# When the SP queue issues the packing loads of an attention kernel, and which engines compute its last inverse deviation

## The chip, the cores and the metric

The kernel runs on one core of one Trainium2 chip. The time is device microseconds of one execution. Each core has five engines with instruction queues of their own: TensorE (PE), VectorE (DVE), ScalarE (ACT), GpSimd (POOL) and SyncE (SP), which here only issues DMAs. Every queue is executed in order; a wait for a semaphore stops all that is queued behind it on that engine.

## The reference

One block for 4 x 1024 tokens of width 256: cross attention (16 heads of 16) over 77 context rows, then a mixture of 8 experts, top one, with a capacity of 640 tokens each.

```python
def reference(x, ctx_1024, mask, Wq, bq, Wk, bk, Wv, bv, Wo, bo, Wr, W1, W2):
    # attention: y = a @ W.T + b, 16 heads, masked softmax, output projection
    x = x + xattn(layernorm(x), ctx_1024, ctx_1024, mask, Wq, bq, Wk, bk, Wv, bv, Wo, bo)
    # experts
    t = layernorm(x).reshape(-1, 256)
    probs = softmax(t @ Wr); idx = argmax(probs); pmax = max(probs)
    pos = position of the token among those of its expert, in order of tokens
    kept = pos < 640
    comb = where(kept, relu(t @ W1[idx]) @ W2[idx], t)
    x = x + comb * where(kept, pmax, 1)
    return x
```

## The kernel before, in words

The tokens are cut into 8 groups (NG) of 512; LAST is 7. The first half of the kernel is a software pipeline over the groups (function `pipeline`): a step has the group `c` whose scores are computed, `n` = c + 1 whose row maxima are taken, `r` = c - 1 whose attention is projected, `o` = c - 2 that is routed, and `a`, `l`, `m` further ahead. The second half goes through the experts; it is TensorE's own work almost without a gap.

The scores of a group are taken in four **rounds** (k or r = 0 to 3). In each, PE multiplies (`scores`, L1439 and L1442), ACT takes the exponentials (L709), PE weighs the values (`weigh_values`, L1475), and ACT copies the unnormalised result of four heads from PSUM to `attnU` (`copy_attn`, L717). Of that strip SP issues three DMAs:

- `gather_sums` (L418) brings the 16 rows of sums of the exponentials to the tile `sums`;
- `store_strips` (L422) writes the whole strip, 256 KB, to DRAM (`strips`);
- `pack_strips` (L429) reads the useful half of it back into `attnC` (`attn_mem` in the trace), with the heads side by side. It must wait for the strip to have landed (`strip_stored`).

When the four gathers of a group have landed, DVE inverts the sums (`invert_sums`, L964), and in the next step SP spreads the reciprocals over the partitions with 8 DMAs (`spread`, L438). DVE multiplies (`normalise_attn`, L970), and PE takes the router's share and projects (`router_of_attn`, L1552, and `project`, L1527). `copy_attn` of round 0 of the next group waits for `sums_loaded` of all four rounds of this one, since it writes over the strip that they are read from; `weigh_values` of round 1 waits for that copy.

The last group (7) does not take this way: PE transposes its strips (`transpose_strips`, L1489, `transpose_back`, L1495).

At the end of the first half, each group's rows are sent to their expert's slots in DRAM. POOL computes the inverse deviation (`second_rstd`, L505 to L550: eight small instructions, with a power of -0.5 and one Newton step), writes it and the mean beside the rows, and issues four indirect DMAs (`dispatch`, L578). For groups 6 and 7 it does rstd, dispatch, rstd, dispatch in a row. DVE computes the slots of a group (`place`, L1075 to L1085), and from the totals the number of tiles of each expert (L1237, L1240), for which PE waits. PE then runs 36 products that keep it busy (KEEP_WARM, L1757), before it transposes the first expert's rows (`transpose_first_pair`, L1687). These come by SP's `load_first_slots` once all rows are sent, and DVE normalises them (L1194). ACT copies the transposed pair (L812), takes the exponential of the first logits (`raise_logits`, L808) and then the first ReLU (L796).

## Time and profile before

| | |
|---|---|
| median of 3 runs | 507.38 us (505.53 to 508.52) |
| the profiled execution | 504.69 us |
| its span, first to last instruction | 503.0 us |
| around the span | 1.69 us |
| PE busy | 463.8 us, 92% |
| DVE, ACT, POOL busy | 41%, 28%, 38% |
| mean granted clock of TensorE | 0.980 |

Times in rows are microseconds from the first instruction, so they add up to the span; a change of the span is set against 504.69, the time of the same execution, and then carried over to the median.

### The profile page before, as it was taken

The page shows a single profiled execution, that of the slowest core. Times are in us where ns is not written, and L with a number is a line of the kernel's source. Part 1 is how long each engine was busy: PE and PEld are TensorE (multiplying, and loading weights), DVE is VectorE, ACT ScalarE, POOL GpSimd, SP SyncE. Part 2 cuts the span into 40 slices and gives each one's busy share as a digit, 9 for nine tenths or more (in the row PEclk, how much of TensorE's full clock was granted, in tenths as well). Part 3 has the DMA queues.
Part 4 walks back from the last instruction along what each step waited for, and adds up shares of the span by engine and source line. Part 5 has one row for each costly group of instructions (what it writes and reads, how often), then busy time and mean ns, then how long its engine had stood idle before and what let it go on. Part 6 is the DMA issues. An engine that isn't in the chain of part 4 may idle for free.

```text
span 503.0 us, 8150 instructions
## 1 busy us (share of the span) xinstructions
PE 463.8 (92%) x3009; PEld 312.4 (62%) x3010; DVE 208.6 (41%) x607; ACT 140.7 (28%) x203; POOL 191.2 (38%) x336
## 2 busy tenths in 40 slices
PE   7999879989999989797947999999999999999995
PEld 3443425334443525142714889989999999899894
DVE  5877436667665646373631331131131131313211
ACT  1135344454535454437201220010010110102000
POOL 5742824465866271827474231101111111131212
PEclk9999999999999999899969999999999999999998
DMA  6998624542434252424115160060240340634000
GB/s 191 308 241 187 220 84 150 149 142 74 155 103 160 88 158 68 156 93 153 53 41 169 55 226 33 18 238 22 66 179 22 115 149 15 236 98 155 19 21 12
DMA packets 49950, 60.66 MB, mean 121 GB/s; under 512 B 4802, under 2 KB 40617, under 8 KB 49904
## 3 DMA queue, kind: packets, MB, share of 16 engines
q1 hardware_dynamic: 42224, 47.49, 31.1%
q0 software_dynamic: 3456, 7.35, 4.3%
q10 hardware_dynamic: 4224, 5.21, 3.4%
q8 instruction: 28, 0.46, 0.4%
q14 instruction: 18, 0.15, 0.1%
HBM read 31.79 MB, written 26.62 MB: 116 GB/s over the span
## 4 chain that ended last, share of the span: by engine, by line
PE 55%; DMA 24%; SPq 12%; issue 3%; POOL 3%; DVE 2%; ACT 1%; POOLq 0%; DVEq 0%; ACTq 0%
DMA strips<-shared 21%; PE tps L1719 11%; PE wk L1729 11%; PE tps L1739 11%; PE wk L1747 10%; SPq L438 6%; SPq L418 3%; SPq L429 3%; PE nat L1296 2%; PE wk L1350 2%; PE nat L1707 1%; PE nat L1417 1%; PE wk L1527 1%; POOL slot_rows L578 1%; PE wk L1475 1%
## 5 line engine op out<-in xcount | busy, mean ns | idle before, releaser
L669 POOL DMA_INDIRECT out_x<-attn_mem,dest x40 | 39.0, 975 | 182.6 <-DVE attn_mem L1261 179.9
L709 ACT ACTIVATE shared<-tps,mask_key 77x1024 f32<-77x1024 f32 x64 | 67.6, 1106 | 27.8 <-PE tps L1442 27.7
L941 DVE TENSOR_REDUCE rowmax<-nat 128x8 f32<-128x616 f32 x58 | 45.9, 791 | 49.2 <-PE nat L1417 49.2
L1729 PE MATMUL wk<-w_sb,shared 128*128 128x256 f32 x256 | 57.7, 379 | 0.0
L1719 PE MATMUL tps<-shared,w_sb 128*128 128x256 f32 x256 | 56.6, 379 | 0.8 <-ACT shared L812 0.8
L1739 PEld LDWEIGHTS tps<-shared,w_sb 128*128 128x128 f32 x480 | 56.0, 192 | 0.8
L1739 PE MATMUL tps<-shared,w_sb 128*128 128x128 f32 x480 | 56.0, 275 | 0.0
L1747 PE MATMUL wk<-w_sb,shared 128*128 128x256 f32 x240 | 54.3, 379 | 0.0
L1719 PEld LDWEIGHTS tps<-shared,w_sb 128*128 128x128 f32 x256 | 48.6, 190 | 7.5 <-issue 1.0
L1729 PEld LDWEIGHTS wk<-w_sb,shared 128*128 128x128 f32 x256 | 48.0, 190 | 6.2
L1417 PE MATMUL nat<-kblk,qT 64*128 64x308 f32 x232 | 46.3, 473 | 4.1 <-DVE rowmax L941 3.8
L1747 PEld LDWEIGHTS wk<-w_sb,shared 128*128 128x128 f32 x240 | 44.5, 190 | 5.4
L1261 DVE SCALAR_TENSOR_TENSOR attn_mem<-wk,gate,x_sb 128x256 f32<-128x256 f32 x31 | 15.0, 484 | 79.1 <-PE wk L1747 41.7
L1475 PE MATMUL wk<-shared,v_ones 77*32 77x512 f32 x256 | 34.9, 618 | 8.9 <-ACT shared L709 8.9
L1417 PEld LDWEIGHTS nat<-kblk,qT 64*128 64x128 f32 x232 | 18.3, 187 | 34.6 <-issue 34.4
L578 POOL DMA_INDIRECT slot_rows<-rows,slot x32 | 32.8, 1025 | 10.9 <-issue 9.3
L505 POOL TENSOR_SCALAR ln<-mv 128x4 f32<-128x4 f32 x16 | 4.0, 251 | 83.2 <-DVE mv L1036 59.5
L1442 PE MATMUL tps<-qT,kblk 32*77 32x512 f32 x256 | 34.2, 610 | 0.0
L802 ACT ACTIVATE shared<-tps 128x512 f32<-128x512 f32 x15 | 9.0, 597 | 88.0 <-PE tps L1739 88.0
L1350 PE MATMUL wk<-xnT,wq_sb 128*128 128x512 f32 x64 | 31.4, 615 | 0.5 <-ACT xnT L689 0.3
L1250 DVE TENSOR_SCALAR shared<-tps 128x512 f32<-128x512 f32 x16 | 11.1, 692 | 46.0 <-PE tps L1719 46.0
L1255 DVE TENSOR_SCALAR shared<-tps 128x512 f32<-128x512 f32 x15 | 10.4, 692 | 46.3 <-PE tps L1739 46.3
(195 smaller groups left out, 556.8 us busy)
## 6 DMA issues: line engine op xcount, KB each, us to landing
w_sb<-in_w SPq DMA_DIRECT2D x12, 1024.0 KB, 8.8
strips<-shared SPq DMA_DIRECT2D x28, 256.0 KB, 3.8
slot_rows<-zeros SPq DMA_DIRECT2D x1, 5340.0 KB, 30.4
x_sb<-slot_rows SPq DMA_DIRECT2D x7, 667.5 KB, 4.4
x_sb<-in_x SPq DMA_DIRECT2D x8, 512.0 KB, 8.8
w_sb<-in_w ACTq DMA_DIRECT2D x4, 1024.0 KB, 7.5
out_x<-base SPq DMA_DIRECT2D x8, 512.0 KB, 3.8
attn_mem<-strips SPq DMA_DIRECT2D x28, 128.0 KB
```

The source lines that it names most:

```text
L578: pool.indirect_dma_start(slots_dram, bass.IndirectOffsetOnAxis(ap=slot[g % 2][:, j:j + 1], axis=0), rows[g % 2][:, j, :], None, bounds_ch ...
L669: pool.indirect_dma_start(out_rows, bass.IndirectOffsetOnAxis(ap=dest[n % 2][:, c:c + 1], axis=0), y_sb[n % 2][:, c, :], None, bounds_chec ...
L709: act.activation(probsT[0:SK, r % 2, 2 * i:2 * i + 2, :], tps[0:SK, 2 * i:2 * i + 2, :], ACT.Exp, bias=mask_key[:, g // GPB:g // GPB + 1]) ...
L941: dve.tensor_reduce(rowmax[:, j, :, m, :], nat_heads(g, k), AX.X, ALU.max).then_inc(rowmax_ready, 1)
L1350: last = pe.matmul(bank[:, :], wq_sb[:, k, m * P:(m + 1) * P], xnT[g % 2][:, k, :], start=(k == 0), stop=(k == KD - 1))
L1417: last = pe.matmul(dst, qT[g % 2][of, m, j * P:(j + 1) * P], kblk[of, b, m, :, :].rearrange("p (i r) k -> p i (r k)", i=2), start=True, st ...
L1442: last = pe.matmul(tps[0:SK, q, :], kblk[of, b, m, (q % 2) * 2 + par, :], qT[g % 2][of, m, :], start=False, stop=True)
L1475: last = pe.matmul(bank[q * QUARTER:(q + 1) * QUARTER, :], v_ones[:, g // GPB, h, :], probsT[0:SK, r % 2, q, :], start=True, stop=True)
L1719: last = pe.matmul(tps[:, quarter, f * two:(f + 1) * two], w1_sb[n % 2][:, k, at * P:(at + 1) * P], tT_slots[n % 2][:, k, 0:two], start=(k ...
L1729: last = pe.matmul(wk[(SC * n + c) % 2][:, 0:D], hidden[:, f, c * P:(c + 1) * P], w2_sb[n % 2][:, f, :], start=(f == 0), stop=(f == FC - 1))
L1739: last = pe.matmul(tps[:, half, f * P:(f + 1) * P], w1_sb[n % 2][:, k, at * P:(at + 1) * P], tT_slots[n % 2][:, k, c * P:(c + 1) * P], sta ...
L1747: last = pe.matmul(wk[(SC * n + c) % 2][:, 0:D], hidden[:, f, 0:P], w2_sb[n % 2][:, f, :], start=(f == 0), stop=(f == FC - 1))
```

## The change

SP's queue is reordered: the packing load of a round stands behind the gather and the store of the round after it, and that of round 3 at the head of the next step, ahead of `spread`. And for group 7 alone the inverse deviation no longer runs on POOL: DVE adds epsilon, ACT takes the square root and copies the mean into the rows, DVE takes a reciprocal and a Newton step, and POOL's `dispatch` waits for these two.

```diff
@@ sync
             def step(m, l, a, n, c, r, o):
                 if has(r):
+                    pack_strips(r, 3)
                     spread(r)
                 if has(o) and o > 0:
                     store_base(o - 1)
@@
                     for k in range(ROUNDS):
                         gather_sums(c, k)
                         store_strips(c, k)
-                        pack_strips(c, k)
+                        if k > 0:
+                            pack_strips(c, k - 1)
 
             pipeline(step)
+            pack_strips(LAST - 1, 3)
             spread(LAST - 1)
@@ gpsimd
             def dispatch(g):
 
-                wait(pool, rstd2_step, 8 * g + 8)
+                if g < LAST:
+                    wait(pool, rstd2_step, 8 * g + 8)
+                else:
+                    pool.wait_ge(last_rstd_ready, 1)
+                    pool.wait_ge(last_mean_ready, 1)
                 wait(pool, route_ready, g + 1)
@@
             second_rstd(LAST - 1)
             dispatch(LAST - 1)
-            second_rstd(LAST)
             dispatch(LAST)
@@ scalar
             copy_attn(LAST, 3)
             copy_back(1)
+            act.activation(std2[:, 0:1], averager[:, 0:1], ACT.Sqrt).then_inc(last_std_ready, 1)
             bias_logits(LAST)
+            act.wait_ge(last_var_ready, 1)
+            act.wait_ge(last_std_ready, 1)
+            act.activation(std2[:, :], var2[:, :], ACT.Sqrt).then_inc(last_std_ready, 1)
+            act.copy(rows[LAST % 2][:, :, MEAN], mv2[:, :, 0]).then_inc(last_mean_ready, 1)
@@ vector
             second_stats(LAST, 1)
             second_moments(LAST)
+            dve.wait_ge(moments2, NG)
+            dve.tensor_scalar(var2[:, :], mv2[:, :, 1], EPS, None, ALU.add).then_inc(last_var_ready, 1)
             masked_positions(LAST)
             place(LAST)
+            dve.wait_ge(last_std_ready, 2)
+            dve.reciprocal(y2[:, :], std2[:, :]).then_inc(last_rstd_step, 1)
+            dve.wait_ge(last_rstd_step, 1)
+            dve.tensor_tensor(yy2[:, :], var2[:, :], y2[:, :], ALU.mult).then_inc(last_rstd_step, 1)
+            dve.wait_ge(last_rstd_step, 2)
+            dve.scalar_tensor_tensor(rstd2[:, :], yy2[:, :], -0.5, y2[:, :], ALU.mult, ALU.mult).then_inc(last_rstd_step, 1)
+            dve.wait_ge(last_rstd_step, 3)
+            dve.scalar_tensor_tensor(rows[LAST % 2][:, :, RSTD], rstd2[:, :], 1.5, y2[:, :], ALU.add, ALU.mult
+                                     ).then_inc(last_rstd_ready, 1)
```

The queue of SP in one step, before: the four rounds of group 1 (L418 gather, L422 store, L429 packing load).

```order
L418 DMA sums<-shared 16x1x128 [waits rsum_ready,attnU_ready]
L422 DMA strips<-shared 128x512
L429 DMA attn_mem<-strips 64x1x512 [waits strip_stored0]
L418 DMA sums<-shared 16x1x128 [waits attnU_ready]
L422 DMA strips<-shared 128x512
L429 DMA attn_mem<-strips 64x1x512 [waits strip_stored1]
L418 DMA sums<-shared 16x1x128 [waits attnU_ready]
L422 DMA strips<-shared 128x512
L429 DMA attn_mem<-strips 64x1x512 [waits strip_stored2]
L418 DMA sums<-shared 16x1x128 [waits attnU_ready]
L422 DMA strips<-shared 128x512
L429 DMA attn_mem<-strips 64x1x512 [waits strip_stored3]
```

The same place of SP's queue now (lines are 5 further down: L423, L427, L434).

```order
L423 DMA sums<-shared 16x1x128 [waits rsum_ready,attnU_ready]
L427 DMA strips<-shared 128x512
L423 DMA sums<-shared 16x1x128 [waits attnU_ready]
L427 DMA strips<-shared 128x512
L434 DMA attn_mem<-strips 64x1x512 [waits strip_stored0]
L423 DMA sums<-shared 16x1x128 [waits attnU_ready]
L427 DMA strips<-shared 128x512
L434 DMA attn_mem<-strips 64x1x512 [waits strip_stored1]
L423 DMA sums<-shared 16x1x128 [waits attnU_ready]
L427 DMA strips<-shared 128x512
L434 DMA attn_mem<-strips 64x1x512 [waits strip_stored2]
L434 DMA attn_mem<-strips 64x1x512 [waits strip_stored3]
```

Each packing load went one gather and one store back; the last two stand together, right ahead of the 8 DMAs of `spread`.

DVE behind `place` of the last group, before: the last slots, then the number of tiles (`tiles_used`), then the first expert's rows.

```order
L1082 TENSOR_TENSOR slotf<-first,pos 128x4
L1084 COPY rows<-token_no 128x4 [waits place_step]
L1085 TENSOR_TENSOR slot<-slotf,past 128x4
L1237 TENSOR_SCALAR tiles_f<-wk 128x8 [waits totals_ps]
L1240 SCALAR_TENSOR_TENSOR tiles_f<-wk,tiles_f 128x8 [waits tiles_step]
L1240 SCALAR_TENSOR_TENSOR tiles_used<-wk,tiles_f 128x8 [waits tiles_step]
```

The same place of DVE now (`ln_0` to `ln_4` are var2, y2, yy2, rstd2, std2).

```order
L1098 TENSOR_TENSOR slotf<-first,pos 128x4
L1100 COPY rows<-token_no 128x4 [waits place_step]
L1101 TENSOR_TENSOR slot<-slotf,past 128x4
L1206 RECIPROCAL ln_1<-ln_4 128x4 [waits last_std_ready]
L1208 TENSOR_TENSOR ln_2<-ln_0,ln_1 128x4 [waits last_rstd_step]
L1210 SCALAR_TENSOR_TENSOR ln_3<-ln_2,ln_1 128x4 [waits last_rstd_step]
L1212 SCALAR_TENSOR_TENSOR rows<-ln_3,ln_1 128x4 [waits last_rstd_step]
L1264 TENSOR_SCALAR tiles_f<-wk 128x8 [waits totals_ps]
L1267 SCALAR_TENSOR_TENSOR tiles_f<-wk,tiles_f 128x8 [waits tiles_step]
L1267 SCALAR_TENSOR_TENSOR tiles_used<-wk,tiles_f 128x8 [waits tiles_step]
```

Four dependent instructions came in ahead of the number of tiles.

ACT at the end of the first half now (L728 is `copy_attn`, L732 `copy_back`, L743 `bias_logits`, L828 the first pair's copy). Before, the two table loads and the rows of L794, L798 and L799 are not there.

```order
L728 COPY shared<-wk 128x512 [waits sums_loaded,strip_stored3,attn_ps]
L732 COPY attn_mem<-nat 128x512 [waits attn_back_ps]
L794 ACT_TABLE_LOAD
L794 ACTIVATE ln_4<-averager 128x1
L743 ACTIVATE lgT<-tps,lg_bias 128x128 [waits lgT_ps]
L798 ACTIVATE ln_4<-ln_0 128x4 [waits last_std_ready,last_var_ready]
L799 COPY rows<-mv 128x4
L828 COPY shared<-nat 128x2x256 [waits tT_slots_ps]
L824 ACT_TABLE_LOAD
L824 ACTIVATE raised<-scaled 128x40 [waits scaled_ready]
L812 ACTIVATE shared<-tps 128x512 [waits hidden_ps0,tiles_ready]
```

A table for the square root is loaded ahead of the last `bias_logits`, and the exponential's again ahead of the first `raise_logits`.

## Rows read from the trace of the kernel before

**Rows 1.** The page's part 4: the chain that ended last, by line.

```profile
DMA strips<-shared 21%; PE tps L1719 11%; PE wk L1729 11%; PE tps L1739 11%; PE wk L1747 10%; SPq L438 6%; SPq L418 3%; SPq L429 3%; PE nat L1296 2%; PE wk L1350 2%; PE nat L1707 1%; PE nat L1417 1%; PE wk L1527 1%; POOL slot_rows L578 1%; PE wk L1475 1%
```

**Rows 2.** Timeline of SP, group 4 to 5: start, length, line, DMA.

```profile
146.34 0.54 SPq L429 DMA_DIRECT2D attn_mem<-strips  x1
146.93 0.56 SPq L418 DMA_DIRECT2D sums<-shared  x1
147.52 0.44 SPq L422 DMA_DIRECT2D strips<-shared  x1
...
152.08 5.19 SPq L438 DMA_DIRECT2D attn_mem<-rsum  x8
```

**Rows 3.** Timeline of ACT, same stretch; brackets: idle before, and what ended it.

```profile
144.21 0.59 ACT L717 COPY shared<-wk 128x512 f32<-128x512 f32 x1 [0.44 <-PE wk L1475]
...
151.09 0.59 ACT L717 COPY shared<-wk 128x512 f32<-128x512 f32 x1 [3.01 <-DMA sums<-shared]
```

**Rows 4.** Waits of PE over the whole span: total us, times, longest.

```profile
PE wk L1475 <- ACT shared L709: 8.9, 5, 2.7
```

**Rows 5.** Timeline of PE where the longest of these waits ends, group 6.

```profile
206.60 1.92 PE L1475 MATMUL wk<-shared,v_ones 77*32 77x512 f32 x8 [2.70 <-ACT shared L709]
```

**Rows 6.** Windows, one per group: length; PE, PEld, DVE, ACT, POOL busy; clock; DMA.

```profile
60.60:90.10 29.50, 26.84 (x186) 11.30 (x182) 13.66 (x33) 13.39 (x17) 11.06 (x16) 0.94 0.45 141
90.10:118.10 28.00, 25.27 (x197) 11.32 (x193) 16.98 (x52) 13.24 (x17) 16.37 (x27) 1.00 0.43 127
118.10:143.70 25.60, 25.40 (x197) 11.26 (x193) 17.39 (x52) 13.44 (x18) 19.64 (x35) 1.00 0.37 118
143.70:170.30 26.60, 25.64 (x200) 11.31 (x193) 15.52 (x46) 13.34 (x18) 12.13 (x24) 1.00 0.38 123
170.30:196.50 26.20, 23.88 (x173) 10.04 (x169) 14.53 (x42) 12.78 (x16) 12.13 (x24) 1.00 0.36 116
196.50:224.80 28.30, 23.60 (x169) 9.59 (x165) 14.91 (x42) 12.18 (x16) 15.83 (x28) 0.94 0.38 123
```

**Rows 7.** Timeline of DVE: the normalisation in two groups.

```profile
159.71 1.29 DVE L970 TENSOR_TENSOR attn_mem<-attn_mem 128x512 f32<-128x512 f32 x2 [0.28 <-DMA attn_mem<-rsum]
...
213.77 1.81 DVE L970 TENSOR_TENSOR attn_mem<-attn_mem 128x512 f32<-128x512 f32 x2
```

**Rows 8.** Timeline of SP in group 6: last store, then spread.

```profile
200.47 0.44 SPq L422 DMA_DIRECT2D strips<-shared  x1
...
204.90 5.19 SPq L438 DMA_DIRECT2D attn_mem<-rsum  x8
```

**Rows 9.** Timeline of POOL: last dispatch of group 6, first of group 7.

```profile
256.59 0.97 POOL L578 DMA_INDIRECT slot_rows<-rows,slot  x1 [0.30 <-issue]
...
261.28 1.12 POOL L578 DMA_INDIRECT slot_rows<-rows,slot  x1 [0.79 <-POOL rows L550]
```

**Rows 10.** Timeline of DVE: number of tiles, and the first expert's rows.

```profile
255.89 0.16 DVE L1237 TENSOR_SCALAR tiles_f<-wk 128x8 f32<-128x8 f32 x1
256.09 0.17 DVE L1240 SCALAR_TENSOR_TENSOR tiles_f<-wk,tiles_f 128x8 f32<-128x8 f32 x1
...
270.62 0.74 DVE L1194 TENSOR_SCALAR shared<-x_sb 128x256 f32<-128x256 f32 x2 [14.17 <-DMA x_sb<-slot_rows]
```

**Rows 11.** Timeline of PE: last logits, the warming products, the first transposes.

```profile
249.78 0.27 PE L1559 MATMUL tps<-ident,uT 128*128 128x128 f32 x1
...
259.20 10.44 PE L1757 MATMUL nat<-max_nat,ones 128*128 128x512 bf16 x35 [3.69 <-issue]
271.41 0.66 PE L1687 MATMUL nat<-ident,shared 128*128 128x128 f32 x4 [1.77 <-DVE shared L1194]
```

**Rows 12.** Timeline of ACT: the only table load, and the end of the first half.

```profile
7.09 1.28 ACT L694 ACT_TABLE_LOAD   x1 [7.09 <-issue]
...
246.73 0.59 ACT L721 COPY attn_mem<-nat 128x512 f32<-128x512 f32 x1 [2.97 <-PE nat L1495]
```

**Rows 13.** The chain in order of time: first products that need the first ReLUs.

```profile
280.63 3.46 PE wk L1729 x16
```

More of the change, by code:

```diff
@@ L167, in xattn_moe @@
         var1, y1, yy1, rstd1 = (sb(f"ln1_{i}", [P, TPG]) for i in range(4))
-        var2, y2, yy2, rstd2 = (sb(f"ln2_{i}", [P, TPG]) for i in range(4))
+        var2, y2, yy2, rstd2, std2 = (sb(f"ln2_{i}", [P, TPG]) for i in range(5))
         lgT = sb("lgT", [P, P])
@@ L304, in xattn_moe @@
         rstd2_step = sem("rstd2_step")
+        last_var_ready = sem("last_var_ready")
+        last_std_ready = sem("last_std_ready")
+        last_mean_ready = sem("last_mean_ready")
+        last_rstd_step = sem("last_rstd_step")
+        last_rstd_ready = sem("last_rstd_ready")
         averages_ps = sem("averages_ps")
```

## The prediction

> **What bounds the kernel now.** I read the chain that ended last first. Its largest single entry is no engine: 21% are stores of strips to DRAM, and with SP's own issue time (lines 438, 418, 429) it runs through SP's queue for most of the first half [rows 1]. So the next view is SP's timeline. There the queue never rests of its own accord: a packing load leaves, the next round's gather and store follow within 0.6 us each, and then SP stands still until that store has landed, since the packing load behind it needs it; after round 3 come 8 spreads, 5.19 us of issue [rows 2]. Who suffers? ACT copied round 3 of group 4 at 144.21 to 144.80, so the gather could have been issued at 144.85. It left at 146.93, behind the packing load of round 2. ACT's first copy of the next group waited for these sums until 151.09, 3.01 us [rows 3]. PE's waits show what reaches it: before `weigh_values` of round 1 it stood 8.9 us in 5 places, behind an exponential that was itself late behind that copy [rows 4], the longest time 2.70 us [rows 5]. The windows by group give the size: one group (the third) has no such wait and lasts 25.60 us with PE busy for 25.40, which is PE's floor; the others last 26.6 to 29.5, but for the fifth, which has less work [rows 6]. So PE and SP's loop are almost tied, and SP's loop is the one that is behind.
>
> **Part 1, the packing loads.** Nothing is removed: 28 gathers, 28 stores, 28 packing loads and 56 spreads are issued as before. What moves is the wait. SP now waits for the landing of strip k with the store of strip k + 1 already out, so two landings overlap, and the gather of round 3 finds the queue free. The packing of round 2, which now needs the issue of round 3, and that of round 3 come together ahead of the spreads.
>
> I place one group on this order, with group 4's times. Gather 144.85, store 145.4, packing of round 2 at 146.0 (its strip landed long ago); the strip of round 3 lands 3.9 us after its issue, which is what 147.52 and the spreads' start at 152.08, less one packing issue of 0.6, show [rows 2]: 149.3. Packing of round 3 until 149.9. The sums came 4.1 us after their gather, with a packing load in front of them [rows 2, 3]; so now by 149.0 at the latest, the reciprocal (0.9 us) by 150.5 once DVE has finished the maximum that it has in front. The spreads start at 150.5, not 152.08: 1.5 us earlier. They ended at 157.3 and DVE's normalisation, which waited 0.28 us for them, began at 159.71 [rows 7]. That chain has then 1.5 us to give, and PE asks for about 1.0. It is enough in groups 1 to 5.
>
> The gain by group, against the floor of 25.6 [rows 6]:
> - group 1: 29.5 - 25.6 = 3.9 us. PE was not busy for 29.50 - 26.84 = 2.7 us of it; the rest is clock: the window's clock is 0.94, so for a part of it PE ran at 1.2 GHz and not at 2.4. The stall gone, that goes too.
> - group 2: 28.0 - 25.6 = 2.4.
> - group 3: nothing.
> - group 4: 26.6 - 25.6 = 1.0.
> - group 5: it has no transposes of a further group, so the floor doesn't hold for it; I take its stall alone, which is what the other four leave of the 8.9 us [rows 4]: 8.9 - 2.7 (group 6) - about 2.5, 2.4 and 1.0 in groups 1, 2 and 4 = 0.3.
> - group 6: its stall is 2.70 [rows 5], and its clock 0.94 too: PE was busy for 23.60 us against 23.88 in group 5, though it has one `query` less (some 2.0 us), so 1.7 us of slow clock. 4.4 us in all. But here the chain of the spreads is the next to be late. The last store left at 200.47, the spreads at 204.90 [rows 8]; in the new order the copy of round 3 ended at 197.55, the sums are there by 201.7, DVE is free at 202.3 and has inverted them at 203.2. So the spreads gain 1.65 us. They landed some 2.3 us after their end (157.3 to 159.7, above), that is at 212.4, and the normalisation began at 213.77 [rows 7]: 1.35 of slack. So 3.0 us of the 4.4 can come.
>
> Sum: 3.9 + 2.4 + 1.0 + 0.3 + 3.0 = 10.6 us. Into group 7 nothing more is gained: its copy ends after SP has caught up, and the chain gather, sums, reciprocal, spreads is as long as before.
>
> What the overlap may cost: packing of round 2 now reads while strip 3 is written. The trace doesn't show this pair. Bounds: it costs nothing (the loads of one queue follow one another, and the 16 DMA engines were busy 36 to 45% of these windows [rows 6]), or as much as the part by which the packing load in front held the old gather, some 1 us per group (4.1 us for 8 KB). Half of it would fall into the slack of 0.5 us. I take 0; the upper end is 5 groups by 0.5, 2.5 us.
>
> **Part 2, the last inverse deviation.** On POOL the eight instructions and a semaphore gap lie between the last dispatch of group 6, which ends at 257.56, and the first of group 7 at 261.28. Now the next dispatch can follow as the others do, 0.30 us behind: 257.86, so 3.4 us earlier [rows 9]. DVE's chain is done by then: it begins where the tiles began, at 255.89, and takes a microsecond (below). Then DVE's first normalised rows start at 270.62 - 3.4 = 267.2 and the transposes could at 268.0.
>
> But PE isn't free then. It runs the warming products from 259.20 to 269.64, and the transposes came at 271.41 after 1.77 us of idle [rows 11]. And those products start when the number of tiles is known, for which DVE now has four dependent instructions and an addition in front. A dependent step of this size has a pitch of 0.20 us (255.89 to 256.09) [rows 10]: five of them, 1.0 us. The warming thus ends at 270.65, and the transposes gain 271.41 - 270.65 = 0.75 us, not 3.4. Bounds: -0.5 (steps of 0.3, each wait 0.1 more, and PE's slow clock longer after the longer rest) to 1.77 (the steps hidden). I take 0.7.
>
> ACT gets two table loads. The one row of such a load lasts 1.28 us [rows 12]. The first begins when `copy_back` ends at 247.32, so the table is there at 248.60, the dummy root at 248.8, and `bias_logits` ends by 249.2. PE takes its result at 249.78 [rows 11]: hidden, with 0.6 us to spare. The second stands behind the copy of the first pair (271.41 + 0.66 + 0.6 = 272.7) and ends at 274.0; the ReLUs behind it are needed at 280.63 [rows 13]: hidden by far.
>
> The trace's one load had nothing before it on ACT, so it doesn't show what a switch costs behind running work. The bounds are the one load, 1.28 us, and twice that, 2.56. I take the one load, as the row has it. The Trainium skill speaks against the change here: its page "ScalarE: Activation LUTs", section "What ACT_TABLE_LOAD costs", says that a switch to another set is the load and a drain of about 1.38 us, 2.66 in all. By that rule, as an estimate, the bias would end at 250.6, 0.8 us past the time at which PE takes it, and the part of the sum for the end of the first half would be 0.7 - 0.8 = -0.1; no row here has such a drain.
>
> **Sum.** 504.69 - 10.6 - 0.7 = 493.4 us for an execution like the profiled one. The median of the runs is 507.38, 0.53% above it; carried over, 496.0 us. That is 2.2% less.
>
> **Rivals.**
> - *A longer switch of tables.* At twice the row's load the table is there at 249.9, the dummy root at 250.1 and the bias at 250.5, 0.7 us after PE wants it; PE's two transposes and the projection behind them wait, and DVE's choice, the totals and the warming with them. For it: nothing in the trace excludes an ACT that stands between two tables. Against it: the one row has 1.28. 496.0 + 0.7 = 496.7 us. (The page's rule above is of this kind.)
> - *The packing chain takes over.* DVE and PE wait for the spreads in every group, because sums or strip 3 land later than I take; the spreads then start only some 0.5 us earlier. For it: the slack in group 4 was negative already, 0.28 us of wait [rows 7], and in group 6 I need this term myself. Against: strips landed in 3.9 us with a packing load ahead of them. Half of the gain goes: 501.0 us.
> - *The gather of round 3 is early, and nothing follows from it*, since PE is at its floor in any case and clock or a later wait eats what the stall gives. Then only a part of the two longest waits goes, 1 to 2 us: about 506, the middle of 504.5 to 508. Against it stand the windows: the group without a stall is the shortest of the full ones.
> - *Slower.* The pair of packing loads waits for a strip 3 that lands late because packing 2 reads beside it. It decides from a start of the spreads more than 7.9 us after the end of the copy (152.08 against 144.21 now). If the strip took 8 us, twice what it does, the spreads would start some 9.9 us after the copy, 2 us later than now, and PE would wait for it in six groups: 12 us more than now, less some 2 for the two longest of the old stalls: 507.4 + 10 = 517 us. Against it: in group 4 even a landing of 6 us would leave it level.
>
> **Chances.** My forecast 0.60, the longer table switch 0.14, the packing chain 0.13, nothing follows 0.07, slower 0.06. What a measurement of this kernel can tell from no change is about 0.5%, 2.5 us, so 504.8 to 509.9 is the same. The first three are faster: 0.87; of the fourth I count most as the same, and some of the slower case is small: faster 0.87, same 0.08, slower 0.05. The range: the sum's bounds are 2.5 us up for the overlap and 1.2 up, 1.0 down for the end; the full 1.4 us of group 6 may come after all, and the medians scatter by 1.5 us. That makes 491.5 to 500; to leave out no more than 2 in 10 it has to reach the packing chain's case: 491.5 to 502.
>
> **What would show it.** SP's timeline: the gather of round 3 within 0.1 us of the copy's end, and SP idle for some 8 us before it. PE's waits: the 8.9 us before `weigh_values` behind ACT gone or under 1. Windows of a group of 25.5 to 25.7 us, clock 1.00. In group 6 a wait of PE for the normalisation of about 1 us. At the end: warming products starting 4.4 us after DVE's last slots (3.4 now: 259.20 against 255.8) and the transposes right behind them with no idle, DVE's rows ready before. ACT's bias done before PE asks. It would be wrong if strip stores took over 5 us, if the groups stayed over 26 us without the ACT wait, or if the warming products ended later than 271.4 in the old frame.

## The result, and the profile after

| | before | after |
|---|---|---|
| median | 507.95 us (505.53 to 509.28, 4 runs) | 492.45 us (490.15 to 493.73, 4 runs) |
| the profiled execution | 504.69 us | 491.57 us |
| its span | 503.0 us | 489.8 us |
| mean granted clock | 0.980 | 0.987 |

Ratio 0.9695, 95% interval 0.964 to 0.975: 3% faster. The forecast was 496.0 us with a range of 491.5 to 502. The span is 13.2 us shorter; the sum had 11.3. The same two kernels, run again later with more executions, gave 0.9742 (below). An execution over 1.5% above the fastest of its kernel stands in the range but is left out of the ratio, which concerns one run of one experiment and three of the kernel before beside it.

Part 4 of the page after, the chain that ended last by engine and by line:

```profile
PE 83%; DVE 9%; issue 3%; DMA 2%; SPq 1%; POOL 1%; ACT 1%; ACTq 0%; DVEq 0%; POOLq 0%
PE tps L1746 11%; PE wk L1756 11%; PE tps L1766 11%; PE wk L1774 11%; PE nat L1444 8%; PE wk L1377 5%; PE wk L1502 5%; PE tps L1469 5%; PE wk L1554 5%; DVE rowmax L957 2%; PE nat L1784 2%; PE tps L1466 2%; PE wk L1361 1%; PE nat L1734 1%; DMA mask_u<-in_mask 1%
```

The strips, 21% of the chain before [rows 1], are no longer among its entries. PE stands in their place.

A word on names. "Group 4" in the rows and here is the window from one maximum cast to the next, in which rounds 0 to 2 of group 4 run. Counted off, the gather and the copy of round 3 and the spreads that fall into it are those of group 3 (the first 16 of 28 gathers), and the normalisation too. Where a group itself is meant below, the text says so.

The timeline of SP in the window of group 4, and under it ACT's copy of round 3 there (start, length, line, operation; brackets: idle before and what ended it):

```profile
128.47 0.56 SPq L434 DMA_DIRECT2D attn_mem<-strips  x1
137.62 0.54 SPq L423 DMA_DIRECT2D sums<-shared  x1
138.19 0.44 SPq L427 DMA_DIRECT2D strips<-shared  x1
138.73 2.23 SPq L434 DMA_DIRECT2D attn_mem<-strips  x2
143.26 5.21 SPq L443 DMA_DIRECT2D attn_mem<-rsum  x8
```

```profile
137.00 0.58 ACT L728 COPY shared<-wk 128x512 f32<-128x512 f32 x1 [0.44 <-PE wk L1502]
```

and DVE's inversion of the sums:

```profile
142.30 0.93 DVE L980 RECIPROCAL rsum<-sums 64x128 f32<-64x128 f32 x1
```

SP was free from 129.03 and issued the gather 0.04 us after the copy's end (2.1 us late before, [rows 2, 3]). The two packing loads are one row: the first left at 138.73, the second, a packing issue long (about 0.55), at about 140.4, as soon as strip 3 had landed, 2.2 us after its store. Packing was over at 140.96, but the spreads start at 143.26, with the end of the reciprocal: 6.26 us after the copy's start, 7.87 before (152.08 against 144.21; the forecast's "7.9 us after the end of the copy" is counted from its start too).

The windows of groups 1 to 6, from one maximum cast of ACT (L715) to the next; columns as in [rows 6], where the last two are the share of the DMA engines and their GB/s:

```profile
59.73:84.99 25.26, 25.13 (x186) 10.91 (x189) 13.16 (x30) 13.47 (x17) 11.65 (x17) 1.00 0.59 194
84.99:110.31 25.32, 25.28 (x197) 11.36 (x200) 16.98 (x53) 13.47 (x18) 16.64 (x27) 1.00 0.39 129
110.31:135.98 25.67, 25.45 (x197) 11.28 (x200) 17.38 (x52) 13.46 (x17) 19.58 (x35) 1.00 0.38 127
135.98:161.29 25.31, 25.27 (x197) 11.35 (x200) 15.41 (x46) 13.47 (x17) 12.35 (x25) 1.00 0.39 128
161.29:186.60 25.31, 23.84 (x173) 10.03 (x177) 14.47 (x43) 12.99 (x16) 12.40 (x24) 1.00 0.38 123
186.60:214.23 27.63, 23.54 (x169) 9.73 (x173) 15.57 (x43) 12.31 (x16) 15.80 (x28) 0.94 0.35 114
```

Cut at the same casts, the kernel before had 29.46, 28.07, 25.64, 26.52, 26.23 and 28.34 us. The gains are 4.20, 2.75, 0, 1.21, 0.92 and 0.71: 9.8 us. Group 6 still has a clock of 0.94. Its rows on PE, and under them DVE's normalisation and POOL's addition of an output bias:

```profile
196.16 1.07 PE L1502 MATMUL wk<-shared,v_ones 77*32 77x512 f32 x8 [1.58 <-ACT shared L720]
197.15 0.48 PE L1466 MATMUL tps<-maxT,minus_piece 32*77 32x512 bf16 x4
197.41 1.93 PE L1469 MATMUL tps<-qT,kblk 32*77 32x512 f32 x8
...
205.59 0.65 PE L1579 MATMUL wk<-attn_mem,wowr_sb 128*32 128x128 f32 x16 [1.36 <-DVE attn_mem L986]
```

```profile
203.21 2.33 DVE L986 TENSOR_TENSOR attn_mem<-attn_mem 128x512 f32<-128x512 f32 x2
...
203.76 3.72 POOL L549 TENSOR_TENSOR x_sb<-x_sb,bo_sb 128x256 f32<-128x256 f32 x4
```

Two things stand out. L1469 takes 1.93 us for eight products that take 1.03 elsewhere: TensorE at 1.2 GHz instead of 2.4. And the normalisation takes 2.33 us where it takes 1.28 in the windows before, while POOL's addition runs beside it; PE waits 1.36 us for it. The end of the first half, on PE:

```profile
242.69 0.19 PE L1597 MATMUL wk<-onehot,before 128*128 128x32 bf16 x1 [1.16 <-DVE onehot L1079]
...
249.21 9.30 PE L1784 MATMUL nat<-max_nat,ones 128*128 128x512 bf16 x36 [3.82 <-issue]
258.34 0.60 PE L1714 MATMUL nat<-ident,shared 128*128 128x128 f32 x4
```

the same stretch on DVE (last slots, first and last step of the new chain, number of tiles, first rows):

```profile
245.69 0.23 DVE L1101 TENSOR_TENSOR slot<-slotf,past 128x4 int32<-128x4 f32 x1
245.76 0.17 DVE L1206 RECIPROCAL ln<-ln 128x4 f32<-128x4 f32 x1
...
246.38 0.17 DVE L1212 SCALAR_TENSOR_TENSOR rows<-ln,ln 128x4 f32<-128x4 f32 x1
...
246.85 0.17 DVE L1267 SCALAR_TENSOR_TENSOR tiles_used<-wk,tiles_f 128x8 int32<-128x8 f32 x1
256.73 0.74 DVE L1221 TENSOR_SCALAR shared<-x_sb 128x256 f32<-128x256 f32 x2 [9.71 <-DMA x_sb<-slot_rows]
```

and on ACT:

```profile
236.38 0.58 ACT L732 COPY attn_mem<-nat 128x512 f32<-128x512 f32 x1 [2.98 <-PE nat L1522]
236.98 1.28 ACT L794 ACT_TABLE_LOAD   x1
238.28 0.20 ACT L794 ACTIVATE ln<-averager 128x1 f32<-128x1 f32 x1
238.38 0.35 ACT L743 ACTIVATE lgT<-tps,lg_bias 128x128 f32<-128x128 f32 x1
```

Against the kernel before, PE is 10.04 us earlier at the last cast, 10.35 at L1597, 9.99 at the first warming product and 13.07 at the transposes [rows 11]. The stretch from the first warming product to the transposes is 9.13 us instead of 12.21: the warming takes 9.30 instead of 10.44, and the 1.77 us of idle behind it are gone. So from L1597 on the end gives 2.7 us, and the rest of the program 0.1: 13.2 in all.

### The profile page after: what moved, and what is told of

The parts are those of the page before. It is cut to its first block, busy times and chain, and to the rows that moved or that the text cites. A ratio compares the mean times of both kernels' runs of the same rounds, so it can differ in the third digit from the quotient of the medians.

```text
span 489.8 us, 8154 instructions
## 1 busy us (share of the span) xinstructions
PE 459.0 (94%) x3010; PEld 311.9 (64%) x3010; DVE 209.7 (43%) x612; ACT 144.3 (29%) x208; POOL 189.5 (39%) x328
## 4 chain that ended last, share of the span: by engine, by line
PE 83%; DVE 9%; issue 3%; DMA 2%; SPq 1%; POOL 1%; ACT 1%; ACTq 0%; DVEq 0%; POOLq 0%
PE tps L1746 11%; PE wk L1756 11%; PE tps L1766 11%; PE wk L1774 11%; PE nat L1444 8%; PE wk L1377 5%; PE wk L1502 5%; PE tps L1469 5%; PE wk L1554 5%; DVE rowmax L957 2%; PE nat L1784 2%; PE tps L1466 2%; PE wk L1361 1%; PE nat L1734 1%; DMA mask_u<-in_mask 1%
## 5 line engine op out<-in xcount | busy, mean ns | idle before, releaser
L1444 PEld LDWEIGHTS nat<-kblk,qT 64*128 64x128 f32 x232 | 18.4, 187 | 34.3 <-issue 34.0
L1469 PE MATMUL tps<-qT,kblk 32*77 32x512 f32 x256 | 33.8, 602 | 0.0
```

Of the source, the lines that this page charges most:

```text
L1444: last = pe.matmul(dst, qT[g % 2][of, m, j * P:(j + 1) * P], kblk[of, b, m, :, :].rearrange("p (i r) k -> p i (r k)", i=2), start=True, st ...
L1469: last = pe.matmul(tps[0:SK, q, :], kblk[of, b, m, (q % 2) * 2 + par, :], qT[g % 2][of, m, :], start=False, stop=True)
```

## The experiments

The kernel before was run again beside each set; ratios are to those runs, with 95% intervals. Edits are shown against the kernel after, cut at `...`. Each experiment has one trace; what is read from it is one execution.

**The order alone** (part 1 without part 2; the last deviation on POOL as before):

```diff
             dispatch(LAST - 1)
+            second_rstd(LAST)
             dispatch(LAST)
...
-            act.activation(std2[:, 0:1], averager[:, 0:1], ACT.Sqrt).then_inc(last_std_ready, 1)
...
-            dve.reciprocal(y2[:, :], std2[:, :]).then_inc(last_rstd_step, 1)
...
```

> SP's queue in the new order, the last inverse deviation on POOL as before. Theory A (the groups' stalls behind SP are 9.8 us of the profiled difference, the end 2.7 us, of which 1.8 is PE's idle before the first transposes): this gives 9.8 to 10.5 us against before, PE idles again some 1.8 us ahead of the first transposes, and group 6 still stands 1.6 us before weigh_values of round 1 with a slow clock behind it. Rival B (the order alone gives all of 13 to 15 us, and the end follows from it): the ratio is that of the full change, 0.970. Rival C (the two parts help each other, the order alone gives half): under 7 us.

Measured: 495.83 us (491.71 to 497.9), ratio 0.9819 [0.9768, 0.9871]. PE's wait for ACT's exponential before `weigh_values`, 8.9 us in 5 places before, is down to 1.6 us in one (L1478 in this kernel). The transposes come 12.16 us after the first warming product, as before (12.21). PE waits for the first rows at the end:

```profile
PE nat L1690 <- DVE shared L1197: 2.5, 1, 2.5
```

The order gives most of the gain, some 9 us of the median, and it alone leaves the end as it was: its warming products are over in 9.67 us, and PE then stands idle 2.5 us instead of 1.8. Group 6 takes 25.05 us at full clock behind the wait of 1.6 us; the slow clock that was expected there came in group 1, which takes 27.86 us.

**The root alone** (part 2 without part 1):

```diff
-                        if k > 0:
-                            pack_strips(c, k - 1)
+                        pack_strips(c, k)
...
```

> The last inverse deviation on DVE and ACT, SP's queue as before. Theory A: 2 to 3 us faster than before: the transposes follow the warming products without idle (1.8 us), these start 0.4 to 0.9 us later, and run 0.5 to 1.3 us shorter if PE's clock goes back to 2.4 GHz sooner. Rival D (0.7 us, as predicted; the rest of 2.7 us in the first comparison was chance of the clock): 0.3 to 1.0 us. No table switch is seen to cost more than 1.28 us.

Measured: 502.24 us (499.13 to 504.11, 12 runs), ratio 0.9957 [0.9927, 0.9987]: 0.4%, some 2 us. The idle behind the warming is gone here too; warming to transposes is 10.41 us instead of 12.21, 1.8 less, since the warming itself took 10.57. That fits the first theory, but the interval, 0.7 to 3.7 us, reaches down to the second. The trace also shows how the old order spends what PE gains elsewhere. PE in group 7:

```profile
236.62 0.82 PE L1576 MATMUL nat<-attn_mem,wowr_sb 128*32 128x128 f32 x16 [3.24 <-DVE attn_mem L983]
```

In this execution the windows of groups 2 to 6 took 25.3 to 25.7 us each, after a first one of 32.13 us (a wait of 3.87 and slow clock), and then PE met the normalisation of the real group 6 3.24 us too early. PE and SP's queue are nearly tied in the old order: PE can run at its own pace for some windows, and pays elsewhere. From the first spreads to the last, six windows on, it is 155.6 us here and 159.7 and 157.5 in the two traces of the kernel before; in the two of the full change it is 152.1 and 150.4. The last spreads start at 227.43, 230.17 and 225.85 in the old order, at 219.21 and 220.40 after the change.

**Only round 2's packing load deferred** (those of rounds 0 and 1 stay where they were):

```diff
-                        if k > 0:
-                            pack_strips(c, k - 1)
+                        if k < 2:
+                            pack_strips(c, k)
+                        if k == 3:
+                            pack_strips(c, 2)
```

> As the full change, but the packing loads of rounds 0 and 1 stand in their old place; only that of round 2 goes behind the gather and store of round 3, and that of round 3 to the next step. Theory A (what pays is that the gather of round 3 finds the queue free): as the full change within 0.5%, if SP can catch up during the 9 us before round 3; SP then has the old two landings in rounds 0 and 1, 4 to 5 us each, and is behind by 1 to 3 us at round 3 in the worst group. Rival E (the overlap of the landings of all rounds pays): only half of the 10 us of the order comes, and PE's waits behind ACT stay at 3 us or more.

Measured: 492.08 us (489.87 to 494.55), ratio 0.976 [0.9714, 0.9807], level with the full change. So the part of the order that pays is the one ahead of round 3. This kernel has both kinds of store in one group; SP's timeline in rounds 1 to 3 of the real group 6:

```profile
208.46 0.56 SPq L423 DMA_DIRECT2D sums<-shared  x1
209.06 0.44 SPq L427 DMA_DIRECT2D strips<-shared  x1
213.27 0.54 SPq L434 DMA_DIRECT2D attn_mem<-strips  x1
213.85 0.56 SPq L423 DMA_DIRECT2D sums<-shared  x1
...
217.75 0.45 SPq L427 DMA_DIRECT2D strips<-shared  x1
218.30 2.15 SPq L434 DMA_DIRECT2D attn_mem<-strips  x2
220.54 5.21 SPq L443 DMA_DIRECT2D attn_mem<-rsum  x8
```

The store at 209.06 had a packing load right ahead of its gather (207.85) and its own packing load went 4.2 us later. The store at 217.75 had none ahead for 4 us: 2.15 us, counting the second of the merged pair as the last 0.55 us of its row. The trace of the kernel before had such a pair too, which the forecast did not use. There the stores of round 0 of groups 1 and 2 stand behind spreads and a gather:

```profile
76.42 0.44 SPq L422 DMA_DIRECT2D strips<-shared  x1
78.55 0.54 SPq L429 DMA_DIRECT2D attn_mem<-strips  x1
```

2.13 us, and 2.17 in group 2; its round 3 stores of groups 1 to 5, each behind a packing load, took 3.7 to 4.8.

**The full change again:** no edit.

> The full change once more, on the chip and in the call of the three below. All theories: 12.5 to 15.5 us under before (ratio 0.970 to 0.976). Theory G (its runs fall into those in which PE's clock drops in group 6 behind its 1.6 us wait and those in which it doesn't): the runs with a mean clock of 0.990 or more are 2 to 4 us shorter than those with 0.986 or less.

Measured: 490.27 us (489.86 to 494.61), ratio 0.9742 [0.9694, 0.9791]. Four runs of mean clock 0.991 lie at 489.9 to 490.3, two of 0.984 and 0.982 at 493.2 and 494.6. The profiled one is slow elsewhere than the first: group 6 took 25.05 us at full clock, though PE waited the same 1.58 us there, and group 1 took 27.84. Windows of this execution (cut at round times), and DVE and POOL in its group 6:

```profile
58.50:86.30 27.80, 27.67 (x198) 10.97 (x198) 12.59 (x28) 13.59 (x17) 13.88 (x18) 0.88 0.47 157
187.00:212.50 25.50, 22.45 (x168) 9.67 (x169) 14.62 (x43) 12.32 (x15) 14.92 (x28) 1.00 0.39 128
```

```profile
205.44 1.28 DVE L986 TENSOR_TENSOR attn_mem<-attn_mem 128x512 f32<-128x512 f32 x2
...
207.60 2.77 POOL L549 TENSOR_TENSOR x_sb<-x_sb,bo_sb 128x256 f32<-128x256 f32 x4
```

PE is busy for nearly all of group 1, so the 2.6 us over the 25.26 of the other execution is clock and no wait. In group 6 the drop of the first execution costs 2.6 us too (27.63 against 25.05), but only 1.5 of it is PE at the slow clock. The other 1.0 is a wait: with PE late, DVE's normalisation began 16.6 us after the cast instead of 15.1 and came to lie beside POOL's addition, which began at 17.2 in both; PE stood 1.36 us before L1579 instead of 0.32. Over the thirteen traces the normalisation of this window took 1.81 to 2.36 us in the four in which the two overlap (both of the kernel before, that of the late store, and the first of the full change) and 1.28 or 1.29 in the nine in which they don't.

Where the clock drops can be counted over the nine traces that have the order of this change (two of the full change, seven of the experiments): in group 6 once, in the execution shown first; in group 1 three times (27.84, 27.86 and 27.78 us against 25.3); in the other five in neither. The mean clock with a drop in group 1 is 0.984 in the two kernels that also have the root, with one in group 6 0.987.

**Filling PE's last wait.** In group 6 there is no `query` to run while ACT takes the exponentials; ten warming products stand in:

```diff
                     if has(a):
                         query(a, 0, c)
+                    else:
+                        keep_warm(10)
                     weigh_values(c, 1, l, n, r, o)
```

> The full change with 10 products that compute nothing, put where group 6 has no query for PE, ahead of weigh_values of round 1. Theory G: PE's wait of 1.6 us there becomes 0 to 0.3, the group lasts as long as before (25.0 us) or 0.2 more where the clock held, and the runs with the low clock become rarer: median 0.5 to 2 us under the full change, clock of the group 1.00. Rival H (group 6 is bound by the spreads, as the prediction had it): PE's wait moves to the normalisation, and the clock drops there.

Measured: 491.58 us (490.23 to 492.98), ratio 0.9757 [0.9713, 0.9802]; the 0.5 to 2 us under the full change did not come. The wait went from 1.58 to 0.17 us and the group still took 25.05 us: products that only fill a wait shorten nothing, since ACT's exponential ends when it did. Three of six runs have a mean clock of 0.984 and no trace. That is the value of the traces with a drop in group 1, where this kernel changes nothing, so these runs do not say what the fill does to the clock of group 6. The three traces with the fill keep it there, but so do five of the six with the order and without the fill.

**Number of tiles ahead of the deviation** (DVE's four new steps moved behind L1267):

```diff
             place(LAST)
-            dve.wait_ge(last_std_ready, 2)
-            dve.reciprocal(y2[:, :], std2[:, :]).then_inc(last_rstd_step, 1)
...
+            dve.wait_ge(last_std_ready, 2)
+            dve.reciprocal(y2[:, :], std2[:, :]).then_inc(last_rstd_step, 1)
...
```

> The full change with DVE's three instructions for the number of tiles ahead of its reciprocal and Newton step. Theory A (the warming products' end is what bounds the first transposes now): the products start 0.7 to 0.8 us earlier, and so do the first transposes, by 0.7 to 0.8 us, until the rows are normalised (0.9 us before the transposes in the full change); 0.8 us faster than the full change. Rival F (the rows' arrival bounds it): no difference, and PE idles 0.8 us before the transposes.

Measured: 489.97 us (489.32 to 494.55), ratio 0.9749 [0.97, 0.9798], not to be told from the full change; the 0.8 us did not come. The last step to the number of tiles starts at 244.66, 0.1 us ahead of the deviation's first (244.75), and PE starts 2.5 us after it:

```profile
247.18 9.82 PE L1783 MATMUL nat<-max_nat,ones 128*128 128x512 bf16 x36 [3.31 <-issue]
```

The products take 9.82 us instead of 9.30, and the transposes follow the last cast by 44.49 us, as in the full change (44.11 and 44.51 in its two traces). A warming product lasts up to 0.63 us at the slow clock and 0.38 in the median; the slow ones were more here, and that ate the earlier start (0.5 to 1.0 us, counted from L1597).

**Thirty warming products instead of 36:**

```diff
-KEEP_WARM = 36
+KEEP_WARM = 30
```

> The full change with 30 warming products for 36. Theory A (the end of these products bounds the first transposes): six at 2.4 GHz are 1.3 us; the transposes come 0.8 us sooner, against DVE's slots, since the rows are normalised 0.9 us before them, and PE idles some 0.4 us. Rival F (rows' arrival bounds): the transposes don't move and PE idles 1.3 us before them.

Measured, one execution: 489.1 us. The transposes come 43.31 us after the last cast, and the products take

```profile
248.01 8.02 PE L1784 MATMUL nat<-max_nat,ones 128*128 128x512 bf16 x29 [4.30 <-issue]
```

with no idle behind them (one record of the thirty is missing). So after the change the warming itself is what ends last there, as forecast, and fewer of the products bring the transposes 0.8 to 1.2 us nearer, in single traces. How few would do, and at what clock the transposes would then run, no run shows.

**Tiles first, the fill of group 6, and POOL's last output bias moved to the end of its step's loop:**

```diff
-                if c == LAST - 1:
-                    add_output_bias(LAST)
             pipeline(step)
...
             rows_kept(LAST - 2)
+            add_output_bias(LAST)
```

> Three edits on the full change: tiles ahead of the Newton step, the 10 products in group 6, and GpSimd's addition of the output bias for group 7, which ran beside DVE's normalisation of group 6 (2.33 us for 1.28), moved behind the rows of group 5. If all three theories hold: 0.8 for the tiles, 0.5 to 2 for the products, 0.5 to 1.0 for the normalisation: 2 to 3.5 us under the full change, normalisation of group 6 back at 1.3 us. If the normalisation's length is no port that GpSimd holds, it stays at 1.8 to 2.3 us.

Measured: 490.18 us (489.62 to 491.01), ratio 0.9728 [0.9687, 0.977]. All six runs have a clock of 0.988 or more; none is at 0.982 to 0.984, as two of the full change's are. Six runs of this, against a full change with two of six dropped, are too few to call the clock held; the median is that of the full change's runs at 0.991. The 2 to 3.5 us under the full change that all three were to give did not come. The normalisation of group 6 takes 1.28 us here, but so it does in every trace of the order without a drop in that window, the bias in its old place: the move would pay only where PE is late there, and this trace does not show such an execution.

**The early gather without the early store.** Packing load k - 1 between gather k and store k:

```diff
                         gather_sums(c, k)
-                        store_strips(c, k)
                         if k > 0:
                             pack_strips(c, k - 1)
+                        store_strips(c, k)
```

> As the full change, but each round's store stands behind the packing load of the round before, and only the gather is ahead of it. Theory I (two things pay: the gather of round 3 that finds the queue free, and that strip 3 lands in 2.1 us for 3.8 because no packing load is right ahead of it): the sums come as early as in the full change, but strip 3 lands some 3.7 us after its issue again, the spreads start 5.5 to 6 us after the copy of round 3 for 3.4 to 5; the groups have slack for it, group 7 has none: PE waits 2 to 3 us for the normalisation there. 1.5 to 3 us slower than the full change. Rival J (the landing was short by chance or by what lies behind the store, not by what lies ahead): strip 3 lands in 2.1 us here too, and the time is that of the full change.

Measured: 508.32 us (506.42 to 515.78, 9 runs), ratio 1.0086 [1.0051, 1.012]: 0.9% slower than the kernel before, though part 2 is in it, and some 17 us slower than the full change where 1.5 to 3 were expected. SP's timeline, last round of the real group 6:

```profile
228.21 0.55 SPq L423 DMA_DIRECT2D sums<-shared  x1
228.86 0.55 SPq L434 DMA_DIRECT2D attn_mem<-strips  x1
229.45 0.45 SPq L427 DMA_DIRECT2D strips<-shared  x1
233.89 0.56 SPq L434 DMA_DIRECT2D attn_mem<-strips  x1
234.55 5.21 SPq L443 DMA_DIRECT2D attn_mem<-rsum  x8
```

Each store stands behind the packing load of the strip before, and in round 3 each strip is then ready 4.4 to 4.6 us after its store. The spreads begin 6.3 us after that gather, against 4.26 before and 3.35 in the full change. DVE stands 13.1 us in 5 places for the spreads (2.6 in 3 before), so the slack that the groups were thought to have was not there. PE's waits:

```profile
PE wk L1579 <- DVE attn_mem L986: 5.5, 2, 3.9
PE nat L1579 <- DVE attn_mem L986: 3.5, 1, 3.5
```

The wait for the sums is gone, and one for the normalisation stands in its place, with the slow clock beside it (0.94, 0.94 and 0.82 in the windows of groups 1, 2 and 6): the early gather is worth nothing unless the store, and with it the spreads, comes early too.

**A version made of the pieces** (30 products, the fill, the bias moved, and six warming products where group 0 meets group 1; the deviation as in the full change):

```diff
-KEEP_WARM = 36
+KEEP_WARM = 30
...
+                        keep_warm(6)
```

> The full change with 30 warming products for 36, the output bias of group 7 moved on GpSimd, and products that compute nothing in PE's two longest rests of the first half: 10 in group 6, and 6 ahead of the last but one natural scores of the step between groups 0 and 1, where one trace has the clock at 1.2 GHz for some 4 us and another not. Theory G: no run with a mean clock under 0.988, all within 1.5 us, median 488 to 489.5, that is 1 to 2.5 us under the full change. Rival K (the clock falls whatever PE does in these places): some runs at 0.984 still, median 490 or more.

Measured: 490.93 us (488.82 to 493.36), ratio 0.976 [0.9722, 0.9797]: no better than the full change. One run has a clock of 0.993, the other five 0.983 to 0.986. In the profiled one, the fastest at 488.82 us, both places that dropped before are at full clock; the end of the first half isn't: the 30 products took

```profile
246.86 8.88 PE L1786 MATMUL nat<-max_nat,ones 128*128 128x512 bf16 x30 [3.94 <-issue]
```

0.86 more than in the other kernel with thirty. The forecast of 488 to 489.5 us and no run under 0.988 was missed: the pieces don't add up, and the slow clock is still there. Where it falls in the other five runs no trace shows.

**The kernel before, under a new name:** no edit.

> The kernel before once more, for a second trace. Theory A (SP's queue is the bound, and PE's waits only move): the spreads of group 6 start at 227 to 230.5 us whatever the groups between do, SP stands only behind its own stores, and PE's waits behind it, in whichever group they fall, group 7's normalisation included, come to 8 to 12 us with the slow clock. Rival L (the waits of the first trace are particular to it): PE's waits are under 4 us and the spreads of group 6 start by 222.

Measured: 504.5 us (500.19 to 506.98, 10 runs), ratio 1.0006 [0.9973, 1.0038]. This is what "no change" looks like here. In its trace, of the fastest execution (500.19 us), the last spreads start at 225.85, with PE's waits elsewhere than in the first (groups of 25.26, 26.51, 25.66, 25.70, 25.91 and 29.92 us), and PE's wait before `weigh_values` is 3.6 us in 3 places, not 8.9 in 5. Neither theory holds as it was put: the queue is later than the rival said, the waits are shorter than the first said. A group's wait in one trace of the old order is a sample and not a constant.

## Why the prediction was right, and where not

**What bounds.** SP's queue, through the wait of a packing load for its own strip. Shown: the order alone gives 0.9819; with it PE's wait for ACT's exponential, 8.9 us in 5 places [rows 4], is 1.6 us in one; and the order with the late store gives all of it back.

**Groups 1 to 5.** Forecast 3.9, 2.4, 0, 1.0, 0.3; measured 4.20, 2.75, 0, 1.21, 0.92. The mechanism and four of the sizes held. The floor was slightly lower than the 25.60 of the third group (25.3), and group 5's stall had been taken as a remainder of the others. That they agree so well is in part because the sizes were read from the very execution they are compared with: against the second trace of the kernel before, the same windows gain 0, 1.2, 0, 0.4 and 0.6. The start of the spreads, 6.29 us after the copy, came out at 6.26. One of its terms was wrong without harm: strip 3 landed in 2.2 us, not 3.9, but the spreads waited for DVE's reciprocal (until 143.23), and that term was right. The 3.9 was read from a store with a packing load right ahead [rows 2], the very thing that the change takes away; the kernel with one deferred load shows 4.2 and 2.15 us side by side, and the trace before had 2.13 at 76.42. Of the cost allowed for the overlap, 0 to 2.5 us, nothing shows: the store ahead of a packing load landed faster, not slower.

**Group 6.** Forecast 3.0, measured 0.71 in the profiled execution and 3.29 in the second trace of the full change (28.34 to 25.05). The failed step is the one that took the whole stall of 2.70 us for SP's, let the slow clock go with it, and named the spreads as what comes next. Of the 2.70 us, 1.58 are not SP's: PE waits them for ACT's exponential in every trace with the order and without the fill. So the stall gives 1.12. The slow clock cost 1.64 us before (from L1475 to the next L1417 it is 3.84 us instead of 2.20; the forecast's 1.7 was right), and the wait for the normalisation beside POOL's addition another 0.53 (0.85 instead of 0.32), which the forecast did not have as a term: 1.12 + 1.64 + 0.53 = 3.29. In the profiled execution the clock fell again (1.5 us) and the normalisation met POOL's addition again (a wait of 1.36), which leaves 0.71. The spreads came 7.31 us after the cast instead of 8.97, 1.66 us earlier as forecast (1.65), and DVE did not wait for them, so the term for them, 1.4 us, was not needed. That its 3.0 is near the 3.29 of an execution without the drop is luck: the 1.4 us kept back for the spreads stand for the 1.58 that ACT keeps. The drop came in this window in one of nine traces; what decides it stays open.

**Into group 7.** Forecast 0. The spreads start 3.35 us after the gather instead of 4.26, because of the shorter landing, and PE's wait for them is 0.3 us instead of 0.65. A gain of 0.3.

**The end.** Forecast 0.7 within -0.5 to 1.77; measured 2.7, outside these bounds. Counted from L1597 (L1570 before) to the transposes it is 18.1 to 18.4 us in three traces without the root (two of the kernel before, one of the order alone), and 15.6 to 16.2 in six of 36 products with the order and the root: 1.8 to 2.7 us. The mechanism was right: the dispatches moved by about 3.4 (247.50, 0.30 behind the one before), the warming became what ends last, the idle of 1.77 went. Two terms were mis-sized. The five steps on DVE were reckoned at 1.0 us. The four that stand ahead of the tiles put them 0.7 us further behind the last slots (246.85 after 245.69, against 256.29 after 255.82), and the first product came 0.36 later in this pair (10.35 gained at L1597, 9.99 there), 3.5 us after DVE's last slots, where I had 4.4. The rest is scatter: from the end of the number of tiles to PE's start it is 2.2 to 2.7 us over all traces, 2.7 in the one before and 2.2 in the one after. And the warming took 1.14 us less. I had held its 10.44 us for a constant, though it contains a stretch at the slow clock that differs from trace to trace: 10.20 to 10.57 in the three with the old order, 9.29 to 9.82 in those of 36 products with a new one, the root or not (9.67 in the order alone). So by these traces, one for each kernel, the 1.1 us go with the order and not with the root; why, none of them shows. It may also be why the two parts alone give less than both (0.9819 by 0.9957 is 0.9777, against 0.9742): with the order alone the shorter warming turns into idle, 2.5 us, and with the root alone the warming stays long. But that gap is within the intervals.

**The table switch.** The rival had 1.28 to 2.56 us. The load stands at 236.98, 0.02 us behind the copy, and the root at 238.28: 1.28 and 0.02 us, also behind running work. The bias ended at 238.73, and PE took it at 239.42: hidden. The second load, behind the copy of the first pair, took 1.28 us as well (259.58, the exponential at 260.88), and the first ReLU behind it still waited 0.66 us for PE. The estimate from the Trainium skill, page "ScalarE: Activation LUTs", section "What ACT_TABLE_LOAD costs" (load and drain, 2.66 us), is not what these rows show.

**The other rivals.** The packing chain did not take over: DVE waited for the spreads in none of the windows of groups 1 to 6 (1.7 us in the window of group 7, 2.0 before), and its 12.3 us of waits for sums, in six places before, are 0.7 in one. "Nothing follows" fell with the windows. "Slower" named strips that land too late behind packing loads. It did not happen in this order, as the store is issued ahead of the load; in the order with the store behind it did, at 4.4 us a strip and not at 8, and that kernel is 0.9% slower than the one before.

**The sum.** 11.3 us forecast, 13.2 measured: 0.3 ahead of group 1, 1.5 more in groups 1 to 5, 2.3 less in group 6, 0.3 into group 7, 2.0 more at the end, 0.1 behind it. So the total is nearer than its parts: 2.3 us too much in group 6 and 2.0 too little at the end cancel, and that is luck. The median fell by 15.5 us, not 13.1: the profiled execution of before was one of its shortest (504.69 against 507.95), that of after lies near its median (491.57 against 492.45). Over the later sets the kernel before has medians of 503.5 to 505.05 us, so the 2.6 us by which the forecast was carried over to the median were not borne out, and the full change, at 490.27 us there, gains 13.2 us and lies below the range. Its lower end is not the sum of its terms either: 496.0 less 1.0, 1.4 and 1.5 is 492.1, not 491.5.

## What to carry to other kernels

Where a queue must wait for a write to land before it reads it back, issue the next item's gather and store first, and check that the store has no read right ahead of it: here the store's place behind an equally early gather decided between a ratio of 0.9742 and one of 1.0086. Don't take a landing time from a row whose neighbours the change removes. And when the bound is a queue, PE's waits wander between groups: read the queue's own pace (first spread to last), and take a group's wait from more than one trace before it is a term of a sum. Ask of each wait how much of it another engine would keep: of 2.70 us here ACT kept 1.58.

## What the runs showed that I had not expected

- A 256 KB store of a strip is ready for its packing load 2.1 to 2.3 us after its issue in round 3 when no packing load was issued right ahead (groups 1 to 6 of the nine traces with the order, but for one of 3.7 in group 1 of the kernel with one deferred load). In the kernel before and with the late store it takes 3.0 to 4.8 us there with a packing load right ahead, though that load moves half as much, and 2.14 in the one case where it was 3.3 us ahead. It is not only these loads: the stores of round 0 behind a 512 KB store of `store_base` take 2.7 to 4.6 us, in the traces before and after, and those behind the spreads 2.1 to 2.2. The runs don't say whether it is the queue's order or the engines that are shared.
- TensorE's clock falls in some executions of one and the same kernel and not in others (full change: 0.991 in four of six, 0.982 to 0.984 in two). Its two traces show two places. In group 6 it falls behind a wait of 1.58 us of PE, which five other traces have without a drop. In group 1 the slow products begin at about 59.6 us, 2.6 us after a wait of 0.99 us that ends at 57.03, and the traces without the drop have that wait too.
- A slow clock of 1.5 us cost 2.6, because DVE's normalisation then met an addition on POOL: 2.33 us instead of 1.28, and POOL's addition 3.72 instead of 2.77.
- A table load behind running work cost ACT its 1.28 us and 0.02 us more, twice.
